# Shared experts' weights stored by partition, a bias wait moved behind the first weight copies, and a three-operand normalisation on VectorE

## The reference

```python
x = x + _L0_ffn_ref(_layernorm(x)[None], Wr, br, W1, b1, W2, b2, gamma, beta)[0]

# in _L0_ffn_ref: D = 128, F = 256, E = 8 experts, K = 2
logits = mean(x, axis=1) @ Wr + br              # one row for all 4096 tokens
routing = softmax(softmax(logits) * scale)
top_w, top_i = top_k(routing, 2); top_w = softmax(top_w)
h = gelu(x @ W1[e] + b1[e]); y[e] = h @ W2[e] + b2[e]
out = layer_norm(sum over the two chosen e of top_w[e] * y[e] + x) * gamma + beta
```

## Time and profile before

| what | value |
|---|---|
| median of 3 runs | 892.39 us |
| lowest, highest | 887.04, 893.5 us |
| the profiled execution: its own time | 889.89 us |
| its span, from first to last instruction | 888.1 us |
| around the span | 1.79 us |
| granted TensorE clock, mean | 0.907 |
| TensorE, VectorE, ScalarE, GpSimd busy | 81%, 66%, 53%, 22% of the span |

### The profile page before, as it was taken

How to read it: one execution, slowest core, us unless ns; L and a number is a source line. 1 busy time by engine, 2 the same in 40 slices (tenths; PEclk the granted TensorE clock), 3 DMA queues, 4 the chain that set the end, 5 groups by cost and what they waited for, 6 DMA issues and landing times. The chain is left out here.

```text
span 888.1 us, 11394 instructions
## 1 busy us (share of the span) xinstructions
PE 721.2 (81%) x3372; PEld 422.0 (48%) x3372; DVE 587.4 (66%) x1691; ACT 471.3 (53%) x695; POOL 195.0 (22%) x233
## 2 busy tenths in 40 slices
PE   2748999999999999999729954699999865687840
PEld 1643444444444444444318843454454454576730
DVE  7785668787878788788757687645465662443424
ACT  1746888888888888888635451313113231222210
POOL 2240000000000000000006422003454347466660
PEclk9978999999999999999959986799999966799885
DMA  4108989998899998878240000300011032232218
GB/s 134 62 0 252 305 259 259 256 268 254 259 262 264 258 260 256 264 236 256 74 125 1 1 1 7 111 10 25 28 35 38 25 80 74 60 85 77 75 32 283
DMA packets 104620, 124.57 MB, mean 140 GB/s; under 512 B 9950, under 2 KB 82914, under 8 KB 104560
## 3 DMA queue, kind: packets, MB, share of 16 engines
q1 hardware_dynamic: 100016, 115.32, 45.3%
q0 software_dynamic: 4544, 8.54, 3.0%
HBM read 88.54 MB, written 36.20 MB: 140 GB/s over the span
## 5 line engine op out<-in xcount | busy, mean ns | idle before, releaser
L552 DVE SCALAR_TENSOR_TENSOR probs<-adj,probs 128x1024 f32<-128x1024 int32 x128 | 156.7, 1224 | 76.8 <-ACT probs L525 73.6
L475 PE MATMUL ps<-x,qT 128*128 128x512 f16 x768 | 188.8, 383 | 3.2 <-PEq L198 3.2
L525 ACT ACTIVATE probs<-ps 128x1024 f32<-128x1024 f32 x128 | 131.1, 1024 | 51.7 <-PE ps L475 51.7
L536 ACT ACTIVATE mask<-probs 128x1024 fp8e4<-128x1024 f32 x128 | 134.0, 1047 | 0.0
L487 PE MATMUL ps<-probs,v 128*128 128x512 f32 x256 | 130.7, 592 | 0.0
L1376 PE MATMUL ps<-mask,parts 128*128 128x512 fp8e4 x512 | 119.3, 389 | 7.4 <-DVE parts L1640 7.4
L475 PEld LDWEIGHTS ps<-x,qT 128*128 128x128 f16 x768 | 75.7, 99 | 95.4 <-issue 6.7
L1623 POOL DMA_INDIRECT mixed_spill<-mask,xn x78 | 76.1, 976 | 53.1 <-issue 27.7
L558 DVE TENSOR_TENSOR p_lo<-probs,p_hi 128x512 f16<-128x512 f32 x128 | 87.5, 684 | 0.1
L1550 ACT ACTIVATE mask<-ps,mask 128x256 f32<-128x256 f32 x78 | 32.5, 472 | 98.4 <-remote 45.9
L1576 POOL DMA_INDIRECT sorted_rows_spill<-rows,slots x64 | 63.1, 986 | 98.5 <-issue 54.1
(11 more groups left out here) (277 smaller groups left out, 969.8 us busy)
## 6 DMA issues: line engine op xcount, KB each, us to landing
adj<-in_adj SPq DMA_DIRECT2D x128, 512.0 KB, 5.0
sorted_rows_spill<-blank SPq DMA_DIRECT2D x32, 528.0 KB, 6.7
sorted_rows_spill<-blank SPq DMA_DIRECT2D x26, 198.0 KB, 7.5
xn<-sorted_rows_spill SPq DMA_DIRECT2D x39, 132.0 KB
mask<-mixed_spill SPq DMA_DIRECT2D x8, 512.0 KB, 5.9
mask<-in_x SPq DMA_DIRECT2D x4, 512.0 KB, 5.8
feat_spill<-mask SPq DMA_DIRECT2D x8, 256.0 KB
x_feat<-in_x SPq DMA_DIRECT2D x8, 256.0 KB, 5.1
```

The source lines that it names most:

```text
L475: ins = nc.tensor.matmul(out, qT[:, q_half, j], kT[:, c, k_half * GROUP:(k_half + 1) * GROUP], start=(n == 0), stop=(n == 2))
L525: nc.scalar.activation(probs[:, k % RING, :], ps[:, b:b + 2, :].rearrange("p b n -> p (b n)"), ACT.Exp, scale=1.0 / QK_SCALE ** 2).then_in ...
L536: nc.scalar.activation(mask[:, k * W:(k + 1) * W], probs[:, k % RING, :], ACT.Sign, saturate=False).then_inc(mask_kept, 1)
L552: nc.vector.scalar_tensor_tensor(out=probs[:, k % RING, :], in0=adj[:, k % LOADS, :], scalar=0.0, in1=probs[:, k % RING, :], op0=ALU.is_gt ...
```

## The change

Five edits, all in `mix_shared_experts` and in the host's table of arrays.

1. `W1a`, `b1a` and `W2a` are transposed on the host so that what a partition receives lies in one piece: 8 KB for `w1_all` (before, 8 pieces of 1 KB), 8 KB for `w2_all` (before, 16 pieces of 512 B in two DMAs), 64 B for `b1_all` (before, 8 pieces of 8 B).
2. `w2_all` comes in one DMA, so VectorE waits for 32 on `experts_in`, not 48.
3. The DMA of `b1_all` stands ahead of that of `w2_all`.
4. ScalarE waits for `small_in` (the biases) behind the two `w1_hi` copies and the third exponential, no longer ahead of them.
5. VectorE's `normalize` is `x1 * rstd + shift` (scalar_tensor_tensor, with shift spread over the row as the second tensor) in place of `(x1 - mean) * rstd` (tensor_scalar).

```diff
@@ block.sync
-                sp.dma_start(w1_all[:, :, :], io["W1a"].rearrange("e d f -> d e f")).then_inc(w1_in, 16)
-                for f in range(FH):
-                    sp.dma_start(w2_all[:, :, f, :], io["W2a"].rearrange("e (f p) d -> f p e d", p=P)[f]).then_inc(experts_in, 16)
-                sp.dma_start(b1_all[:, :, :], io["b1a"].rearrange("e p f -> p e f")).then_inc(small_in, 16)
+                sp.dma_start(w1_all[:, :, :], io["W1a"]).then_inc(w1_in, 16)
+                sp.dma_start(b1_all[:, :, :], io["b1a"]).then_inc(small_in, 16)
+                sp.dma_start(w2_all[:, :, :, :], io["W2a"]).then_inc(experts_in, 16)
@@ block.vector, normalize
-                        ins = nc.vector.tensor_scalar(xn[:, t, :], x1[:, t, :], mean[:, t:t + 1], rstd[:, t:t + 1], ALU.subtract, ALU.mult)
+                        ins = nc.vector.scalar_tensor_tensor(out=xn[:, t, :], in0=x1[:, t, :], scalar=rstd[:, t:t + 1],
+                                                             in1=shift[:, t:t + 1].to_broadcast([P, D]), op0=ALU.mult, op1=ALU.add)
@@ block.vector
-                dve.wait_ge(experts_in, 48)
+                dve.wait_ge(experts_in, 32)
@@ block.scalar
                 act.wait_ge(w1_in, 16)
-                act.wait_ge(small_in, 16)
                 act.wait_ge(index_ready, 1)
...
                 exponential(3, route_exp[:, 0:2], share[:, :])
+                act.wait_ge(small_in, 16)
@@ kernel, on the host
-        "W1a": L0_ffn_W1, "b1a": np.asarray(L0_ffn_b1).reshape(E, FH, P).transpose(0, 2, 1), "W2a": L0_ffn_W2, "b2a": L0_ffn_b2,
+        "W1a": np.asarray(L0_ffn_W1).transpose(1, 0, 2), "b1a": np.asarray(L0_ffn_b1).reshape(E, FH, P).transpose(2, 0, 1),
+        "W2a": np.asarray(L0_ffn_W2).reshape(E, FH, P, D).transpose(2, 0, 1, 3), "b2a": L0_ffn_b2,
```

## The result

| | before | changed |
|---|---|---|
| median of the runs | 893.22 us (22 runs, 885.29 to 895.78) | 886.81 us (22 runs, 883.12 to 891.12) |
| ratio, 95% interval | | 0.9943, 0.9924 to 0.9962 |
| profiled execution, its span | 889.89, 888.1 us | 887.86, 886.0 us |
| stage of the change, from its first DMA issue to the next stage's | 89.93 us | 85.89 us |
| granted TensorE clock, mean | 0.907 | 0.907 |

The account below looks back on a forecast made before the run. It took TensorE's wait for w1_lo, caused by the biases' DMA, as the bound; TensorE's path gains 4.0 + 0.46 = 4.5 us, VectorE's 3.9, the smaller counts: 889.89 - 3.9 = 886.0, median 2.5 above, 888.5 us, range 882.5 to 893.5.

Parts of the forecast that it names:

- What bounds: Start of the stage: TensorE's one long wait, 8.4 us for w1_lo, goes back through ScalarE to the biases' DMA.
- First matmul, a gain of 4.0: First up-matmul: without the bias wait it starts at 459.8 instead of 463.82, a gain between 3.6 and 4.4 us.
- w1's landing: DMA of w1: lands 7.1 us after issue or a little less; W1b's 5.8 us was the bound.
- w2's scaling, a gain of 3.9: VectorE's w2 scaling: starts at 460.5, when w2 and b2 have landed, a gain of 2.5 to 4.4 us.
- Edit 5, nothing: VectorE's eight normalising instructions: the three-operand form stays held by GpSimd's adds at 9.05 us, so it gains nothing.
- The smaller of two paths: Into up(2): TensorE's path gains 4.5 us, VectorE's 3.9; the stage gains the smaller.
- The wait before up(2): TensorE before up(2): still waits for xT_lo, by about 1 us.
- The total: Whole kernel: profiled execution 886.0 us, median 888.5 us, range 882.5 to 893.5; this forecast's chance 0.58.
- rival D: Whole stage: the loads don't matter, another wait takes the 4 us back, 892 us; chance 0.08.
- A: Normalising instructions: the new form is free of GpSimd, TensorE's path decides, gain 4.5 us, 887.9 us; chance 0.19.
- B: Load at the stage's start: w1 lands with w2, a gain of 0.9 us only, 891.5 us; chance 0.12.
- C: Load at the stage's start: long pieces move slowly, w2 scaling moves to 474.8, total 902.8 us; chance 0.03.

Follow-up runs that it names:

- e9: Changed kernel with the old normalising form, normalize(3), (4) ahead of the bias row, two GpSimd waits and add_outputs(4) moved on VectorE: stage 81.06 us, ratio 0.9905.
- e10: Changed kernel with tensor_scalar again, normalize(3), (4) in their old place, two GpSimd waits and add_outputs(4) moved on VectorE: stage 81.45 us, ratio 0.9905.
- e6: Changed kernel with the old tensor_scalar normalisation put back: stage 84.09 us, ratio 0.9943.
- e1: Kernel before with only ScalarE's wait for the biases moved behind the w1 copies: stage 86.91 us, ratio 0.9970.
- e4: Kernel before with only the biases' DMA, still 1,024 pieces of 8 bytes, issued ahead of w2: stage 88.64 us, ratio 0.9948.
- e7: Changed kernel with shift for groups 3 and 4 copied to PSUM, so eight normalising instructions read one SBUF tensor: they take 2.15 us, stage 83.33 us, ratio 0.9919.
- c1: The changed kernel again, unaltered, on a third chip where the kernel before takes 857 and 856 us: stage 85.89 us, ratio 0.9935.
- e5: Changed kernel with ScalarE's wait for the biases put back ahead of the w1 copies: stage 84.34 us, ratio 0.9957.
- e3: Kernel before with only the new layout and w2 in one DMA, biases' DMA still last, wait in its old place: stage 86.34 us, ratio 0.9943.

## Why the prediction was right, and where its terms were off

- *What bounds.* Right. The wait for w1_lo went from 8.4 to 3.9 us, of which none is the biases'; TensorE is the engine that is full behind it, and VectorE's path into up(2) sets the rest. "Its one long wait there" passed over a second one: TensorE waits 3.0 us for ScalarE before up(7), before as in the changed kernel, and e9 and e10, which cut it to 0.7, gained 2.6 us of stage (e10 against e6) that no part of this change reached.
- *First matmul, a gain of 4.0 (3.6 to 4.4).* It was 4.45, just outside the stated bounds. The term that was mis-sized is w1's landing: I put it "near the row of this very transfer", 7.1 us and a little off, and it was 6.0 (in the old layout it was 6.6 in e1 and 7.0 in e4, so a part of the 7.1 was that one execution's). The row of W1b (5.8), which I used as the bound, was the better one. The indices were last, as that bound had it, at 6.3, and with 1.49 us of index reading w1_hi stood at 7.79.
- *w2's scaling, a gain of 3.9 (2.5 to 4.4).* It was 4.45, again outside, and VectorE did not wait for b2, which landed at 9.9 where I had 10.7. I took out only the gap of the tiny pieces; that the long pieces would run at 385 to 467 GB/s, above the 369 that I took as the best rate, was left out, and it put the landing below my earliest bound (10.1).
- *Edit 5, nothing.* It costs 0.38 us of VectorE's path (9.43 against 9.05; e6 has 9.06). That it does not get past GpSimd was right, and e7 shows the reason to be the second tensor from SBUF. This agrees with the Trainium skill ("SBUF — State Buffer", Who interferes with whom), by which a VectorE instruction with two SBUF inputs contends with a GpSimd one that reads SBUF, and one with at most one SBUF input does not, as long as it is outside the fast two-port modes. I bounded the edit by zero from below; that GpSimd's adds would be stretched, and with them the turns that VectorE waits for, was missed: the eight adds go from 9.9 us to 10.3 (463.23 to 473.5).
- *The smaller of two paths.* TensorE was ready 4.08 us earlier, which with the old slack of 0.46 makes 4.5; VectorE gained 4.45 - 0.38 = 4.07. VectorE's counts, and the stage gave 4.04. That the smaller path decides was right; that the sum came so near to 3.9 was luck, two errors of 0.5 and 0.4 us with opposite signs. TensorE's 4.5 was as forecast by luck too: the first matmul gained 0.45 us more, and the longer start at the low clock, which I had left out behind 463.82, took 0.37 back. The wait before up(2), "about 1 us", was 0.47 (0.79 in c1, 0.16 in e5); my own terms, 0.46 and a TensorE path 0.1 us ahead, made 0.6.
- *The total.* The time was 886.81 us and the forecast 888.5. The profiled execution, forecast at 886.0, took 887.86: outside the stage it was 2.0 us longer than before. The range of 882.5 to 893.5 also holds no gain at all (892 in rival D), so the total alone would not have told the forecast from its rivals; the marks do. The ratio's interval, 3.4 to 6.8 us, holds the 4.0 of the stage; c1's, 0.9917 to 0.9953, is 4.0 to 7.1 us of 856 and holds it only at its edge. Something up to 1 or 2 us beyond what one profile shows may be there, for instance in how often TensorE's clock falls in the late part. The 22 runs of the changed kernel have a mean granted clock of 0.911 and the 31 runs of the kernel before beside e1 to e4 one of 0.907, where the profiled executions of the two have 0.907 both; 4 us less at the low clock make some 0.002 of that difference (4 x 0.5 / 890, an estimate). The rest stays open.
- *The rivals.* A (the form is free) is refuted by 9.43 us. B and C (w1 late, long pieces slow) are refuted by the landings and rates: longer pieces were faster. D did not happen.
- *What I did not see at all:* that the edits overlap. e1 gives 2.8 us at z, e3 gives 2.1, e4 gives 2.4, the whole 4.1. With the new layout and order the moved wait is worth nothing (e5).

## What to carry to other kernels

Price a wait by what lands last once it is gone: moving the wait for the biases brought 2.8 us and then met the load behind it, and moving the biases' DMA forward in the new layout made the moved wait superfluous. VectorE beside a GpSimd add of two SBUF tensors was not helped by another instruction alone, but by where its second tensor lies or by when it runs; a two-tensor instruction of 8 columns can cost 1.3 us there, and two semaphore waits on GpSimd, with one call moved on VectorE to fill the time, were worth 2.6 us (a stage of 81.5 us in e10 against 84.1 in e6), where the three-operand edit cost 0.4. Compare marks within a stage, counted from its start, when the effect is 0.4 us and the executions of one kernel differ by up to 10.

## What the runs showed of the hardware that I had not expected

- An issue's length followed what stood ahead of it in the queue more than what it issued: the same 1,024 pieces of 8 bytes took 4.28 us behind w2 and 0.58 us ahead of it (e4), and w2's issue went from 2.10 to 5.37 us.
- The load with 8 KB in one piece for a partition moved at 385 to 467 GB/s in windows of 1 us (334 to 467 in c1, 380 to 442 in five of e3's), where the one with pieces of 1 KB and 512 B reached 369 at best and 312 on average in six windows from its best one on (the kernel before).
- Held VectorE instructions and GpSimd's adds took turns, one for one, whatever the form. GpSimd's adds follow each other by 1.25 us beside the one-tensor form, or beside the form with its second tensor in PSUM (462.65 to 465.15 in e7), but by up to 1.30 beside the form with two tensors from SBUF.
- After the same idle time of 3.0 us, the same matmuls ran at a granted clock of 0.61 (c1) in one execution and 1.00 (e5) in another, worth 1.5 us of the stage.
